# Weighted values as columns in tiles of 32, and the keys' norm moved into the exponential's scale

## The chip, the cores and the metric

The kernel runs on one core of a Trainium2 chip. Its engines are TensorE (PE: matmuls and transposes), VectorE (DVE), ScalarE (ACT), GpSimd (POOL) and the queues that issue DMAs (SP's above all). The metric is the time of one execution on the device in microseconds (us). Before the change it is 1096.64 us, the median of three runs (1096.35 to 1097.41).

## The reference, cut to what matters

Sixteen sequences of 256 tokens with 128 features pass four sublayers: a decaying complex convolution, a mixture of eight experts of which two count, attention with sixteen heads, and a mixture of four layers of which two count. Each stands between layer norms and is added to its input. The change lies in the attention, in the reference:

```python
q = (xn @ w_q).reshape(b, n, HEADS, DIM_HEAD).transpose(0, 2, 1, 3)   # 16 heads of 64
k, v = jnp.split(xn @ w_kv, 2, axis=-1)                                # k, v as q
k = jnp.concatenate([nk, k], axis=2)   # two learned "null" keys and values in front
v = jnp.concatenate([nv, v], axis=2)
q = _l2norm(q) * q_scale
k = _l2norm(k) * k_scale
sim = jnp.einsum('bhid,bhjd->bhij', q, k) * 8.0
sim = sim + dist[None, None] * slopes[None, :, None, None]   # by distance, per head
sim = jnp.where(causal_mask[None, None], neg, sim)
attn = jax.nn.softmax(sim, axis=-1)
out = jnp.einsum('bhij,bhjd->bhid', attn, v)
out = out.transpose(0, 2, 1, 3).reshape(b, n, HEADS * DIM_HEAD)
return out @ w_out
```

## The kernel before, in words

The sixteen sequences are taken in eight groups of two; a group is four tiles of 128 tokens, so 512 tokens. The sublayers of different groups overlap: while group i is in attention, the experts of group i+1 and the start of the convolution of group i+2 are woven in, and the last sublayer of group i-1 runs beside the projections of group i.

What each engine does, and in which order, is written out by hand in tables of step names (PROLOGUE, FIRST, MIDDLE, LAST_L, LAST_A, LAST_F), one list for each engine. `plan` plays them: FIRST once, MIDDLE for five groups, then the three last ones. A step a_ belongs to the attention, l_ to the experts, f_ to the last sublayer, e_ to the convolution, s_ to the setup. Engines meet through semaphores only, and each engine runs strictly down its list: a step that waits holds up all that stand behind it.

The attention of one group has these steps:

- a_m.t (L1693 to L1695 on PE, three matmuls of rounded float32 for each product; L1042 and L1049 on ACT): k and q of token tile t are computed into banks 0 to 2, copied to `unit` and squared into `square`.
- a_ss.t.k: DVE sums the squares by head (L1497), k = 0 for keys and 1 for queries, clamps them (L1500), and POOL raises them to the power of -1/2 (L858, `rnorm`).
- a_u.t.k: DVE scales `unit` by `rnorm` (L1506), for the keys and for the queries.
- a_t.t: PE turns the four parts of `unit` (L1700), ACT copies them into `kT` (L1058) and `qT` (L1060), features by tokens.
- a_v.t: the values into `val`, with a column of ones behind each head.
- a_scores.c: for two heads, PE multiplies keys by queries (L1914 for 256 queries, L1920 for 128), with 64 rows each, two tiles of rows side by side. The result has keys as partitions. ACT takes the exponential with the slope as bias by partition and 8 as the scale (L1108, L1111), POOL multiplies the triangle of the mask (L866). The four buffers of probabilities are `probs`, which lie in `unit` and `square`.
- a_mix.h: for one head, six float32 matmuls of 128x128 (L1955, L1957). The probabilities are the stationary operand and the values with their ones, 128 columns wide, move, so tokens are the partitions of the result, in bank 3. DVE adds the null probabilities to the denominator (L1547), inverts it (L1549) and multiplies (L1551) into `mixed`.
- a_oT.c: PE turns two heads of `mixed` back (L1700), ACT copies them to `outT` (L1129); the last one turns the null probabilities (L1997).
- a_out.h: `outT` times w_out (L2010) plus the null probabilities times w_nv, the null values folded with w_out in the setup (L2011).

In the last group, which has no later one to weave in, the order of heads differs: two sequences one after the other, four heads at a time (L1085 and L1090 on ACT).

Among the other rows that are named: L1837 and L1844 belong to the experts, L2043 to L2113 to the last sublayer, L1635 is DVE's second step on its hidden rows.

## Time and profile before

| | |
|---|---|
| median of three runs | 1096.64 us |
| profiled execution: its span | 1095.0 us |
| PE busy | 1008.8 us (92%), 6854 matmul records |
| DVE busy | 790.9 us (72%) |
| ACT busy | 564.5 us (52%) |
| POOL busy | 571.8 us (52%) |

The profiled execution is one of its own; the span of its trace is 1095.0 us, and the median of the runs is 1.6 us longer. The chain of waits is followed back from the last instruction, at each step to what released it. A record of a matmul begins when it starts and its end is modelled, so records overlap, and what one costs in a row of them is the distance of the starts. One float32 matmul shows as two records, one of rounded float32 as one. The granted clock of PE is 1.00 (2.4 GHz) in all stages shown below.

### The profile page before, as it was taken

What the parts mean: (1) busy time and instruction counts of PE and PEld (TensorE: products, weight loads), DVE (VectorE), ACT (ScalarE), POOL (GpSimd) and SP (SyncE); (2) the same over time, 40 slices, a digit from 0 to 9 for tenths busy, and PEclk for the clock granted to TensorE, in tenths of its full rate; (3) what the DMA queues carried; (4) which work ended last, traced back from release to release, by engine and by line L of the source; (5) the groups of instructions that cost most, each with busy time, mean ns of one, the idle gap of its engine ahead of it and who ended that gap; (6) DMA issues with size and microseconds to landing.
All of it is one profiled execution on the core that took longest, in us unless ns stands there. A gap on an engine that the chain in (4) does not pass through costs nothing.

```text
span 1095.0 us, 19137 instructions
## 1 busy us (share of the span) xinstructions
PE 1008.8 (92%) x6854; PEld 833.2 (76%) x6854; DVE 790.9 (72%) x2565; ACT 564.5 (52%) x1113; POOL 571.8 (52%) x562
## 2 busy tenths in 40 slices
PE   0887999899999999999999999999998999999987
PEld 0565888679975989679886789669896788768965
DVE  5787656977689776888578776887678664793446
ACT  5217653764347542773447542574527653486522
POOL 4127543854457463764637553674637643475523
PEclk9988999999999999999999999999999999999999
DMA  6200000000000000000000000000000000000000
GB/s 161 75 1 10 1 1 1 1 11 1 11 1 1 11 1 11 0 11 1 2 11 1 10 1 11 1 10 1 1 11 1 1 1 1 10 1 1 11 1 10
DMA packets 21870, 11.31 MB, mean 10 GB/s; under 512 B 7440, under 2 KB 21136, under 8 KB 21648
## 3 DMA queue, kind: packets, MB, share of 16 engines
q1 hardware_dynamic: 18064, 8.84, 2.9%
q10 hardware_dynamic: 3712, 1.25, 0.5%
q8 instruction: 55, 0.90, 0.3%
q14 instruction: 39, 0.32, 0.1%
HBM read 7.99 MB, written 2.10 MB: 9 GB/s over the span
## 4 chain that ended last, share of the span: by engine, by line
PE 51%; DVE 29%; POOL 14%; issue 5%; ACT 1%; ACTq 0%; DVEq 0%; POOLq 0%
PE bank L1955 10%; POOL rnorm L858 9%; PE bank L1914 5%; PE bank L1957 5%; PE bank L1700 4%; PE bank L1920 3%; PE bank L1693 3%; DVE unit L1506 3%; DVE sumsq L1497 3%; PE bank L1694 3%; PE bank L1695 3%; PE bank L2107 3%; PE bank L2113 3%; PE bank L1844 2%; PE bank L2010 1%
## 5 line engine op out<-in xcount | busy, mean ns | idle before, releaser
L858 POOL TENSOR_TENSOR rnorm<-sumsq,minus_half 128x16 f32<-128x16 f32 x64 | 185.2, 2921 | 9.4 <-DVE sumsq L1500 9.4
L866 POOL TENSOR_TENSOR unit<-unit,causal 128x256 f32<-128x256 f32 x128 | 89.5, 731 | 100.6 <-ACT unit L1111 87.1
L866 POOL TENSOR_TENSOR square<-square,causal 128x256 f32<-128x256 f32 x128 | 89.4, 730 | 96.3 <-ACT square L1111 87.1
L1914 PE MATMUL bank<-qT,kT 64*128 64x256 f32 x512 | 96.8, 389 | 0.0
L1547 DVE TENSOR_TENSOR denom<-bank,null_sum 128x4 f32<-128x4 f32 x112 | 17.8, 159 | 97.6 <-PE bank L1957 97.4
L1506 DVE TENSOR_TENSOR unit<-unit,rnorm 128x1024 f32<-128x1024 f32 x64 | 79.1, 1240 | 11.3 <-POOL rnorm L858 10.9
L1920 PE MATMUL bank<-qT,kT 64*128 64x128 f32 x512 | 84.1, 284 | 0.8 <-ACT val L1066 0.7
L1497 DVE TENSOR_REDUCE sumsq<-square 128x16 f32<-128x1024 f32 x64 | 77.8, 1215 | 7.4 <-ACT square L1049 7.1
L1955 PE MATMUL bank<-val,unit 128*128 128x128 f32 x512 | 81.4, 282 | 1.3 <-DVE mixed L1551 1.0
L1955 PE MATMUL bank<-val,square 128*128 128x128 f32 x512 | 80.9, 281 | 0.8 <-DVE mixed L1551 0.6
L1129 ACT ACTIVATE qT<-bank 128x512 f32<-128x512 f32 x56 | 33.4, 599 | 93.6 <-PE bank L1700 93.5
L1700 PE MATMUL bank<-ident,unit 128*128 128x128 f32 x520 | 71.3, 286 | 10.8 <-DVE unit L1506 8.3
L1042 ACT ACTIVATE unit<-bank 128x512 f32<-128x512 f32 x128 | 72.2, 601 | 17.3 <-PE bank L1695 14.2
L1920 PEld LDWEIGHTS bank<-qT,kT 64*128 64x128 f32 x512 | 71.1, 187 | 12.1 <-issue 5.1
L1700 PEld LDWEIGHTS bank<-ident,unit 128*128 128x128 f32 x520 | 61.0, 147 | 25.4 <-DVE unit L1506 13.4
L1955 PEld LDWEIGHTS bank<-val,unit 128*128 128x128 f32 x512 | 67.6, 191 | 7.9 <-issue 3.8
L1049 ACT ACTIVATE square<-unit 128x512 f32<-128x512 f32 x128 | 72.9, 630 | 0.1
L1955 PEld LDWEIGHTS bank<-val,square 128*128 128x128 f32 x512 | 68.0, 192 | 5.6 <-issue 2.1
L1914 PEld LDWEIGHTS bank<-qT,kT 64*128 64x128 f32 x512 | 68.8, 187 | 0.5
L1108 ACT ACTIVATE square<-bank,bias_k 128x512 f32<-128x512 f32 x56 | 38.2, 683 | 56.9 <-PE bank L1914 56.9
L2010 PE MATMUL bank<-w_out,qT 128*128 128x128 f32 x512 | 64.3, 279 | 1.4 <-ACT tanh L1121 0.7
L1693 PE MATMUL bank<-w_kv_hi,xaT_hi 128*128 128x512 f32 x128 | 62.1, 485 | 2.5 <-DVE xaT_lo L1402 1.5
(396 smaller groups left out, 2798.0 us busy)
## 6 DMA issues: line engine op xcount, KB each, us to landing
xin<-in_L_attn_x SPq DMA_DIRECT2D x7, 256.0 KB, 2.8
out<-x SPq DMA_DIRECT2D x7, 256.0 KB, 2.2
square<-in_L_attn_w_kv SPq DMA_DIRECT2D x1, 1024.0 KB, 7.3
w_sw<-in_L_ffn_sw_w SPq DMA_DIRECT2D x3, 256.0 KB, 5.0
unit<-in_L_attn_w_q SPq DMA_DIRECT2D x1, 512.0 KB, 6.4
w_out<-in_L_attn_w_out SPq DMA_DIRECT2D x1, 512.0 KB, 4.3
w_ml<-in_L_ffn_ml_w SPq DMA_DIRECT2D x2, 256.0 KB, 5.5
xin<-in_L_attn_x ACTq DMA_DIRECT2D x1, 256.0 KB, 3.0
```

The lines of the kernel that those rows point to most:

```text
L858: pool.tensor_tensor(rnorm[:, k, t, :], sumsq[:, t % 2, k, :], minus_half[:], ALU.pow).then_inc(a_root.sem, 1)
L866: m = pool.tensor_tensor(pd, pd, causal[:].unsqueeze(1).to_broadcast([P, 2, P]), ALU.mult)
L1042: act.activation(unit[:, t % 2, i, :], bank[n % 3][:], ACT.Copy).then_inc(a_took.sem, 1)
L1049: act.activation(square[:, k, :], unit[:, t % 2, k, :], ACT.Square).then_inc(a_sq.sem, 1)
L1497: V.tensor_reduce(sumsq[:, t % 2, k, :], square[:, 2 * k:2 * k + 2, :].rearrange("p j (h d) -> p (j h) d", d=DH), AX_X, ALU.add).then_inc( ...
L1506: V.tensor_tensor(raw, raw, rnorm[:, k, t, :].unsqueeze(2).to_broadcast([P, H, DH]), ALU.mult).then_inc(a_unit.sem, 1)
L1693: mm(dst, left.hi, right.hi, start=True, stop=False)
L1700: last = nc.tensor.transpose(dst[:, t * P:(t + 1) * P], src(t), ident[:])
L1914: return mm(bank[s][:, 2 * P * i:2 * P * (i + 1)], kT[rs, p, 2 * P * b:2 * P * b + P], qT[rs, p, 2 * P * b:2 * P * (b + 1)], start=True, s ...
L1920: return mm(bank[2][:, 2 * P * s + P * i:2 * P * s + P * (i + 1)], kT[rs, p, ts], qT[rs, p, ts], start=True, stop=True)
L1955: last = mm(dst, pr[:, i, 2 * k, :], wide_val(2 * b + k, head), start=True, stop=(k == 0))
L2010: mm(out_bank(g, h)[:, ts], outT[:, c, ts], w_out[:, c, :], start=(c == 0), stop=False)
```

## The change

It has two parts.

The first turns the product with the values around. The values become the stationary operand, 32 of their 64 features at a time, and the probabilities move, so that the result comes out as features by tokens, as `outT` needs it. Four heads stand side by side in the columns of the array. One unit (a_mix.c, eight for a group) does four heads of one sequence. The denominator is a product of its own, with 32 columns of ones, in bank 7; the null keys enter by three full-width matmuls with the turned null probabilities (`null_pT`, now 96 rows: one rounded part twice and one rest) and the matrices `of_head` and `w_nv`. DVE turns the denominators by blocks of 32x32, inverts them, turns them back and multiplies into `outT`. The steps a_oT and the matmuls with w_nv in a_out go, and a step a_nT comes, which turns the null probabilities. Since a unit holds one sequence, all groups now take the heads in the order of the last one, with two exponentials where there was one: four heads of one sequence in place of two heads of both.

The second leaves the keys without their norm. a_k.t turns the raw keys; DVE's clamp of the keys' squares also divides by 64, and POOL's root is then eight times the inverse norm, which the exponential takes as its scale by partition.

The tables of the order are written anew for both parts. Buffers move: the tanh rows go to `conv` and `hid_relu`, `null_pT` to `xaT`. In the setup, null heads are spread over `w_nv` by POOL and ACT, w_out is loaded by eight DMAs in place of one, and null values by three.

```diff
-            def a_units(g, t, k):
-                dve.wait_ge(a_root.sem, a_root.at(g, 2 * t + k + 1))
-                dve.wait_ge(a_took.sem, a_took.at(g, use("m", t, 2 * k + 1) + 1))
-                raw = unit[:, t % 2, 2 * k:2 * k + 2, :].rearrange("p j (h d) -> p (j h) d", d=DH)
-                V.tensor_tensor(raw, raw, rnorm[:, k, t, :].unsqueeze(2).to_broadcast([P, H, DH]), ALU.mult).then_inc(a_unit.sem, 1)
+            def a_units(g, t):
+                dve.wait_ge(a_root.sem, a_root.at(g, 2 * t + 2))
+                dve.wait_ge(a_took.sem, a_took.at(g, use("m", t, 3) + 1))
+                raw = unit[:, t % 2, 2:4, :].rearrange("p j (h d) -> p (j h) d", d=DH)
+                V.tensor_tensor(raw, raw, rnorm[:, 1, t, :].unsqueeze(2).to_broadcast([P, H, DH]), ALU.mult).then_inc(a_unit.sem, 1)
...
+                    V.tensor_scalar(sumsq[:, t % 2, k, :], sumsq[:, t % 2, k, :], 1e-24, 1.0 / 64.0, ALU.max, ALU.mult).then_inc(s.sem, 1)
...
-            def a_t(g, t):
+            def a_k(g, t):
...
+                for k in range(2):
+                    n = use("k", t, k)
+                    pe.wait_ge(a_took.sem, a_took.at(g, use("m", t, k) + 1))
                     free(g, n)
                     turn(bank[n % 3], lambda c: unit[:, t % 2, k, c * P:(c + 1) * P]).then_inc(a_put.sem, 1)
...
-                            last = act.activation(pr[:, j, 0:2, :], k0, ACT.Exp, bias=bias_k0[:, h:h + 1], scale=8.0)
+                            last = act.activation(pr[:, j, 0:2, :], k0, ACT.Exp, bias=bias_k0[:, h:h + 1], scale=by)
...
-                for i in range(2):
-                    b, head = (seq_of(h), head_of(h, i)) if ending(g) else (i, h)
-                    for k in range(2):
-                        dst = bank[pv_bank(g, h)][:, (2 * i + k) * P:(2 * i + k + 1) * P]
-                        last = mm(dst, pr[:, i, 2 * k, :], wide_val(2 * b + k, head), start=True, stop=(k == 0))
-                        if k:
-                            last = mm(dst, pr[:, i, 1, :], wide_val(2 * b, head), start=False, stop=True)
-                last.then_inc(a_pv.sem, 1)
...
+            def a_mix_(g, c):
+                b, q = unit_of(c)
+                quad = [(slice(32 * i, 32 * i + 32), QW * q + i, probs[(2 * c + i % 2) % 4][:, i // 2, :, :]) for i in range(QW)]
+
+                def weigh(dst, left):
+                    for rs, h, pr in quad:
+                        mm(dst[rs, P:2 * P], left(1, h), pr[:, 2, :], start=False, stop=False, skip_group_check=True)
+                    for rs, h, pr in quad:
+                        last = mm(dst[rs, :], left(0, h), pr[:, 0:2, :], start=False, stop=True, skip_group_check=True)
+                    return last
+
+                pe.wait_ge(a_mask.sem, a_mask.at(g, 2 * c + 2))
+                if c:
+                    pe.wait_ge(a_mix.sem, a_mix.at(g, 4 * c - 3))
...
+                elif c and not ending(g):
+                    pe.wait_ge(a_mix.sem, a_mix.at(g, 4 * c))
+                den = bank[7][:, 0:2 * P]
+                parts = [pv_bank(g, c)[:, 2 * P * f:2 * P * (f + 1)] for f in range(2)]
+                mm(den, of_head[:, P * q:P * (q + 1)], null_pT[:, half(b)], start=True, stop=False, skip_group_check=True)
+                for f in range(2):
+                    mm(parts[f], w_nv[:, (2 * q + f) * P:(2 * q + f + 1) * P], null_pT[:, half(b)], start=(f == 0), stop=False,
+                       skip_group_check=True)
+                weigh(den, lambda k, h: ones[:]).then_inc(a_den.sem, 1)
+                for f in range(2):
+                    last = weigh(parts[f], lambda k, h: val[:, 2 * b + k, h, 32 * f:32 * f + 32])
+                last.then_inc(a_pv.sem, 1)
...
+            def a_nT_(g):
...
+                for t in range(T):
+                    for i in range(3):
+                        last = mm(bank[3][32 * i:32 * i + 32, t * P:(t + 1) * P], null_p[:, t, :, :].rearrange("p h n -> p (h n)"), ident[:],
+                                  start=True, stop=True)
+                last.then_inc(a_nT.sem, 1)
...
+                V.transpose(den_rows, bank[7][:, 0:2 * P]).then_inc(s.sem, 1)
+                dve.wait_ge(s.sem, s.at(g, 4 * c + 1))
+                V.reciprocal(recip[:], den_rows[:, 0::32]).then_inc(s.sem, 1)
+                dve.wait_ge(s.sem, s.at(g, 4 * c + 2))
+                V.transpose(rec_cols.rearrange("p (n i) -> p n i", i=32), recip[:].unsqueeze(2).to_broadcast([P, 2 * QW, 32])).then_inc(s.sem, 1)
+                dve.wait_ge(s.sem, s.at(g, 4 * c + 3))
+                dve.wait_ge(a_pv.sem, a_pv.at(g, c + 1))
+                V.tensor_tensor(outT[:, 2 * q:2 * q + 2, half(b)], pv_bank(g, c)[:].rearrange("p (f n) -> p f n", f=2),
+                                rec_cols.unsqueeze(1).to_broadcast([P, 2, 2 * P]), ALU.mult).then_inc(s.sem, 1)
...
-                        mm(out_bank(g, h)[:, ts], outT[:, c, ts], w_out[:, c, :], start=(c == 0), stop=False)
-                    last = mm(out_bank(g, h)[:, ts], null_pT[:, ts], w_nv[:], start=False, stop=True)
+                        last = mm(out_bank(g, h)[:, ts], outT[:, c, ts], w_out[:, c, :], start=(c == 0), stop=(c == 7))
```

The order on PE, in the middle of one group's attention: before, the turn of two finished heads (L1700 with `mixed`), two heads' values (L1955, L1957) and a block of scores.

```order
L1700 MATMUL bank<-ident,mixed 128x128 x4
L1955 MATMUL bank<-val,unit 128x128 x2
L1957 MATMUL bank<-val,unit 128x128
L1955 MATMUL bank<-val,unit 128x128 x2
L1957 MATMUL bank<-val,unit 128x128
L1837 MATMUL bank<-coef,sel 128x512
L1920 MATMUL bank<-qT,kT 128x128
L1914 MATMUL bank<-qT,kT 128x256
```

The same place after the change, a unit (L1926 and L1928 are the two loops of `weigh`, L1948 and L1950 the full-width matmuls) and the scores behind it:

```order
L1948 MATMUL bank<-xaT_hi,of_head 128x256
L1950 MATMUL bank<-xaT_hi,w_nv 128x256 x2
L1926 MATMUL bank<-square,ones 32x128 x4
L1928 MATMUL bank<-square,ones 32x256 x4
L1926 MATMUL bank<-square,val 32x128 x4
L1928 MATMUL bank<-square,val 32x256 x4
L1926 MATMUL bank<-square,val 32x128 x4
L1928 MATMUL bank<-square,val 32x256 x4
L1668 MATMUL bank<-ident,xn 128x128 x4
L1783 MATMUL bank<-ident,pick 8x128 x4
L1895 MATMUL bank<-qT,kT 128x128
```

Four heads of one sequence now stand in one piece, and no turn of `mixed` is left.

The order on DVE at the end of the projections, before: after the last squares, the keys' scaling (L1506) stands in front of the residual of the convolution (L1325, L1330) and the queries' behind it.

```order
L1325 TENSOR_SCALAR ce_rows<-ce_rows,n_c_mv,n_c_rstd 128x128 x4
L1506 TENSOR_TENSOR unit<-unit,rnorm 128x1024
L1325 TENSOR_SCALAR xn<-bank,n_y_mv,n_y_rstd 128x128 x4
L1330 TENSOR_TENSOR x<-xn,xin 128x512
L1314 BN_STATS n_l_six<-x 128x6 x4
L1318 BN_AGGR n_l_mv<-n_l_six 128x2 x4
L1320 TENSOR_SCALAR n_l_var<-n_l_mv 128x4
L1506 TENSOR_TENSOR unit<-unit,rnorm 128x1024
```

After:

```order
L1311 TENSOR_SCALAR ce_rows<-ce_rows,n_c_mv,n_c_rstd 128x128 x4
L1311 TENSOR_SCALAR xn<-bank,n_y_mv,n_y_rstd 128x128 x4
L1316 TENSOR_TENSOR x<-xn,xin 128x512
L1300 BN_STATS n_l_six<-x 128x6 x4
L1304 BN_AGGR n_l_mv<-n_l_six 128x2 x4
L1306 TENSOR_SCALAR n_l_var<-n_l_mv 128x4
L1495 TENSOR_TENSOR unit<-unit,rnorm 128x1024
```

One scaling is gone, and the one of the queries stays behind the residual.

## Rows read from the trace of the kernel before

**Rows 1.** The page's shares of the chain of waits by engine, whole span

```profile
PE 51%; DVE 29%; POOL 14%; issue 5%; ACT 1%; ACTq 0%; DVEq 0%; POOLq 0%
```

**Rows 2.** Busy time by stage: stretch, length, then each engine's busy us (instructions), clock, DMA

```profile
488.00:549.00 61.00, 60.92 (x502) 55.19 (x501) 40.62 (x135) 27.58 (x56) 32.48 (x41) 1.00 0.01 1
549.00:569.30 20.30, 20.19 (x146) 17.90 (x145) 15.90 (x68) 6.36 (x13) 4.18 (x6) 1.00 0.05 15
569.30:613.50 44.20, 40.35 (x200) 27.73 (x199) 39.93 (x112) 33.30 (x62) 33.71 (x17) 1.00 0.02 7
```

**Rows 3.** Pieces of the chain of waits: start us, length us, engine and line

```profile
489.81 0.24 PE bank L1695
490.05 0.89 PE bank L2107 x8
...
1073.02 0.86 PE bank L2044 x2
```

**Rows 4.** Timeline of attention: start us, length us, engine, line, operation, tiles

```profile
506.98 0.71 PE L1955 MATMUL bank<-val,unit 128*128 128x128 f32 x4
...
508.34 0.48 PE L1693 MATMUL bank<-xlT_hi,w_gate_hi 128*128 128x512 f32 x1
```

**Rows 5.** Timeline of PE, end of attention and the norms

```profile
550.90 0.60 PE L1700 MATMUL bank<-ident,mixed 128*128 128x128 f32 x4
551.33 1.28 PE L1844 MATMUL bank<-w_down,unit 128*128 128x128 f32 x10
...
556.32 0.48 PE L2011 MATMUL bank<-w_nv,tanh 32*128 32x128 f32 x2
556.74 2.05 PE L2010 MATMUL bank<-w_out,qT 128*128 128x128 f32 x16
```

**Rows 6.** Timeline of PE, one block of scores and its neighbours

```profile
493.49 0.25 PE L1695 MATMUL bank<-w_router_hi,xlT_lo 128*128 128x8 f32 x1
493.67 0.37 PE L1920 MATMUL bank<-qT,kT 64*128 64x128 f32 x1
493.68 0.48 PE L1914 MATMUL bank<-qT,kT 64*128 64x256 f32 x1
493.88 0.38 PE L1920 MATMUL bank<-qT,kT 64*128 64x128 f32 x2
...
494.98 0.27 PE L1920 MATMUL bank<-qT,kT 64*128 64x128 f32 x1
495.18 1.16 PE L2107 MATMUL bank<-w_sw,mixed 128*128 128x128 f32 x8
```

**Rows 7.** Timeline of PE, projections; in brackets its idle time before

```profile
580.64 1.09 PE L1700 MATMUL bank<-ident,unit 128*128 128x128 f32 x8 [0.51 <-DVE unit L1506]
...
604.34 3.03 PE L2066 MATMUL bank<-xmT,w_ml 128*128 128x512 f32 x6 [1.49 <-DVE mixed L1635]
```

**Rows 8.** Groups of DVE by form: tiles, shapes, count, busy us, mean ns, idle before

```profile
L1506 DVE TENSOR_TENSOR unit<-unit,rnorm 128x1024 f32<-128x1024 f32 x64 | 79.1, 1240 | 11.3 <-POOL rnorm L858 10.9
...
L1551 DVE TENSOR_TENSOR mixed<-bank,recip 128x256 f32<-128x256 f32 x112 | 47.6, 425 | 3.9
...
L1635 DVE TENSOR_TENSOR mixed<-mixed,bank 128x512 f32<-128x512 f32 x32 | 22.0, 687 | 1.1
...
L1549 DVE RECIPROCAL recip<-denom 128x4 f32<-128x4 f32 x112 | 20.2, 180 | 3.9
...
L1547 DVE TENSOR_TENSOR denom<-bank,null_sum 128x4 f32<-128x4 f32 x112 | 17.8, 159 | 97.6 <-PE bank L1957 97.4
```

**Rows 9.** Groups of ACT by form, exponentials of the scores

```profile
L1108 ACT ACTIVATE square<-bank,bias_k 128x512 f32<-128x512 f32 x56 | 38.2, 683 | 56.9 <-PE bank L1914 56.9
...
L1085 ACT ACTIVATE square<-bank,bias_k 128x256 f32<-128x256 f32 x16 | 6.7, 474 | 4.8 <-PE bank L1914 4.8
...
L1090 ACT ACTIVATE unit<-bank,bias_k 128x128 f32<-128x128 f32 x16 | 5.2, 395 | 0.0
```

510 lines of the change are left out of this document (214 added, 296 removed).

## The prediction

> **What bounds the kernel now.** I read the stages first [rows 2], cut at the steps of one iteration of the middle loop. It takes 125.5 us and falls into attention (488 to 549 us; the kernel's first MLP layer is woven into it), a run of layer norms (20 us) and the projections of q, k and v (44 us). In attention TensorE (PE) is busy for 60.92 of 61 us; VectorE (DVE) has 40.6, ScalarE (ACT) 27.6, GpSimd (POOL) 32.5. In the projections DVE has 39.9 of 44.2 us and PE 40.4. The chain of waits says the same of the whole: PE carries 51% of it, DVE 29%, POOL 14% [rows 1]. So in attention a microsecond that PE gains or loses counts nearly in full, in the projections only PE's gaps can be won, and in the norms a ping-pong of DVE and POOL sets the pace. There are eight groups of two sequences, so each term is worked out for one group and taken eight times.
>
> The unit of all PE terms is the pass. A float32 matmul shows as two passes; one over 512 columns takes 0.86 / 2 = 0.43 us, one over 128 columns 0.89 / 8 = 0.11 us, so one over 256 about 0.215. A pass of rounded float32 over 512 columns takes 0.24 [rows 3].
>
> **What PE loses.** A head's weighted values, six float32 matmuls, stand from 506.98 to 508.34: 1.36 us [rows 4], sixteen heads 21.8. A turn of the result (four transposes) takes 551.33 - 550.90 = 0.43 us [rows 5]; six of them lie in attention, 2.6. In sum 24.4 us. Three more turns and four matmuls with w_nv (0.42 each, from 556.32 to 556.74 [rows 5]) go from the stretch of norms: 3.0 us.
>
> **What PE gains.** Eight units. In each, three full-width matmuls of rounded float32 over 256 columns (no such row; half of 0.24, so 0.12; bounds 0.11, since no pass in these rows is shorter, and 0.215): 0.36. Then three times the same block, which I call w: four heads side by side in column tiles of 32, each with a float32 matmul over 128 and one over 256 columns. One after the other its passes take 8 x 0.11 + 8 x 0.215 = 2.6 us; four abreast 0.65. No row shows column tiles. The nearest are the scores, with two row tiles of 64: exactly the same set of passes, 2.6 us in a row and 1.30 two abreast. They run from 493.67 to the last start at 494.98 plus 0.11, which is 1.42 us, and their second matmul starts 0.01 us after the first while the first's own second pass comes only at 493.88 [rows 6]. The tiles really run beside each other, at 92% of the ideal. I take w = 0.65 x 1.42 / 1.30 = 0.71, bounds 0.65 and 2.6. Around the scores PE has a hole of 0.07 us before (493.49 + 0.11 to 493.67) and 0.09 behind (495.09 to 495.18) [rows 6]; I take 0.1 for each change of tile size, two in a unit. A unit is 0.36 + 3 x 0.71 + 0.2 = 2.69 us, eight are 21.5. The twelve small matmuls that turn the null probabilities come in threes abreast, 4 x 2 x 0.11 + 0.2 = 1.1. Together 22.6 against 24.4: -1.8 us for a group, -14 for all. At w = 0.65 it would be -26, and at w = 0.79 nothing.
>
> The Trainium skill ("TensorE: Matmul & The Clock Gate", Measured speedup vs the span model) gives 2.38 times for three column tiles. Scaled to four (an estimate, 3.17 times) w would be 0.82, the PE term +7 us and the total 1075. No run here shows column tiles yet.
>
> **Projections.** DVE loses four of the eight scalings by the norm, 4 x 1.24 = 5.0 us for a group [rows 8], and the transposes of k no longer wait for POOL's root. But DVE's time isn't what counts, PE's gaps are, and they come to 44.2 - 40.35 = 3.9 us [rows 2]. The largest wait for DVE: 0.51 for a scaled half in front of its transposes, and 1.49 for a hidden part of the second layer, which stands on DVE behind the scalings [rows 7]. The last link stays, q's scaling in front of q's transposes, and DVE reaches it one scaling, 1.2 us, earlier. I take -2.5 us for a group (bounds 0 and -3.9): -20.
>
> **Norms.** The chain there starts at DVE's last multiplication and passes through units of norm work that don't change. PE loses 3.0 us in it but is only partly waited for. I take -1 (bounds 0 and -3): -8.
>
> **What I cost at nothing.** On DVE a unit has two stream transposes (no such row; bounds 0.18, the reciprocal, and 0.69, a 128x512 operation; I take 0.43, the 128x256 one from the bank), a reciprocal and a multiplication of 0.69: 1.73 us in place of 2 x (0.16 + 0.18 + 0.43) = 1.54 for two heads [rows 8]. That is +1.6 us for a group beside 20 free ones. Two waits come with it. A unit's first matmul waits for the multiplication of the unit before, because both write bank 3, and for its first transpose, because the denominators have bank 7 alone; the turn of the normed input, which shares bank 7, waits likewise. All of PE's queue stands behind such a wait. The multiplication is through about 1 us after a unit's last pass, and scores of 1.5 us stand between any two units but the last two, where half of the down projection does. If that cover went, each unit would cost up to 1 us, 64 in all. On ACT a pair of heads now takes 4 x 0.474 + 4 x 0.395 = 3.5 us of exponentials, before 2 x (0.683 + 0.474) = 2.3 [rows 9], +9 us for a group. Even without the copies of the turned result, which go, that is 37 of 59 us. The scale by partition I take as free, since the bias is already read that way (bounds 0 and 0.1 us for each of 64 exponentials in a group). The prologue loses eight small matmuls and gets seven DMAs and some POOL and ACT work ahead of a wait that comes later: 0, bounds -2 and +2.
>
> **Sum.** -14 - 20 - 8 = -42 us. The profiled span is 1095.0, so 1053; the median of the runs lies 1.6 above it, which gives 1054.6. From here on differences under 0.2% (2 us) are no change, as a measurement can't tell them.
>
> **Rivals.**
> A, two abreast. The passes of a float32 matmul are two instructions, and a second pass must follow the first in its own tile. If PE keeps the order of passes within a row group, tile 1 starts only when tile 0's second pass has, and so on: never more than two at work, w = 1.3. A unit is then 4.46 us, eight 35.7, the PE term +12.4 for a group, with the other gains +8.9 and 71 in all: 1168. It decides from w = 0.79 for PE and 0.93 for the whole. For it: the scores cross row groups, where this can't be seen; all four column tiles share all rows. Against it: in the scores the passes of two matmuls are interleaved, not in order [rows 6]. The Trainium skill's rule speaks for it ("TensorE: Matmul & The Clock Gate", Part 3, The mechanism): matmuls start and end in program order and only weight loads are pulled ahead, when their row group differs. The scores here break it by 0.2 us, across row groups.
> B, a floor per pass. Away from the scores no pass takes under 0.11 us, whatever its size. If 16 passes cost 16 x 0.11, w is 1.8, a unit 5.96, the PE term +24.4, in all +167: 1264. Against it: 16 passes of the scores take 1.42, that is 0.09, with the array full. A floor of 0.06 would give w = 0.96 and +6 in all.
> C, no overlap at all: w = 2.6, a unit 8.36, the PE term +43.6, in all 1417. Against it: row tiles do overlap [rows 6].
> D, the exponentials take PE's place. The scores of a pair wait for all exponentials of the pair before; if PE arrives 0.7 us early at each of eight, +5.6 for a group and +45 in all eat the gain: 1099, next to no change. For it: +1.2 us for a pair on ACT. Against it: a pair has 59 / 8 = 7 us, and a loop of 1.4 us of scores and 3.5 of exponentials is shorter.
>
> **How the numbers follow.** Four abreast has 0.56; its own range is 1031 (w = 0.65, which gives -12 more, and all of the gaps, -11 more) to 1090 (w = 0.85, +27, and a third of the gaps, +9). A has 0.20, B and C together 0.12, D and a small floor 0.12, of which 0.05 is faster, 0.05 no change and 0.02 slower. Predicted is the likeliest, 1054.6, as 1054. The range leaves out B and C and the slow end of A: 1031 to 1172. Faster is 0.56 + 0.05 = 0.61, the same 0.05, slower 0.20 + 0.12 + 0.02 = 0.34.
>
> **What would show it.** The w blocks: twelve or more passes starting within 0.7 us, the first passes of four tiles within a few hundredths. Under A starts come in steps of 0.11 and 0.215 with two open at a time. Attention would take about 59 us and the projections 41.5. PE stays near 99% busy in attention; if it falls and the longest waits are PE's scores for ACT, D holds. The prediction is wrong if w is above 0.93, or if the projections keep their 44 us.

## The result and the profile after

The changed kernel takes 1107.1 us (median of four runs, 1104.4 to 1108.9) against 1096.5: slower by 1%, ratio 1.0092 with an interval of 1.0076 to 1.0108. The profiled execution spans 1104.2 us where that of before spans 1095.0. The forecast was 1054. One of the eleven executions of a later kernel, the column tiles alone, took 3268.5 us where the others took 1092 to 1096, and stands in no comparison.

PE's work fell as planned, and more. On the page of the profile before, it is 1008.8 us busy (92%); after, first lines and chain shares (engine, busy us, share of the span, instructions; then the chain by engine):

```profile
span 1104.2 us, 22172 instructions
PE 964.8 (87%) x8405; PEld 738.5 (67%) x8405; DVE 778.6 (71%) x2393; ACT 617.7 (56%) x1288; POOL 578.9 (52%) x570
PE 50%; DVE 28%; ACT 11%; issue 5%; POOL 5%; ACTq 0%; DVEq 0%; POOLq 0%
```

So PE works 44 us less and stands idle 53 us more (139 for 86). ACT had 1% of the chain [rows 1]; it has 11%.

One unit on PE, from the timeline (start, length, engine and line, tiles, shapes, count); the rows of before for one head are [rows 4], for row tiles [rows 6]:

```profile
516.79 0.28 PE L1948 MATMUL bank<-xaT_hi,of_head 96*128 96x256 f32 x1
516.91 0.40 PE L1950 MATMUL bank<-xaT_hi,w_nv 96*128 96x256 f32 x2
517.24 0.43 PE L1926 MATMUL bank<-square,ones 128*32 128x128 f32 x8
517.48 0.61 PE L1928 MATMUL bank<-square,ones 128*32 128x256 f32 x8
517.91 0.40 PE L1926 MATMUL bank<-square,val 128*32 128x128 f32 x8
518.13 0.61 PE L1928 MATMUL bank<-square,val 128*32 128x256 f32 x8
518.56 0.40 PE L1926 MATMUL bank<-square,val 128*32 128x128 f32 x8
518.78 0.61 PE L1928 MATMUL bank<-square,val 128*32 128x256 f32 x8
519.33 0.33 PE L1668 MATMUL bank<-ident,xn 128*128 128x128 f32 x1
```

A block of sixteen passes begins every 0.65 us (517.91 - 517.24 = 0.67, then 0.65), and the trace has the first passes of its four tiles within 0.02 us of each other. The four tiles work abreast with nothing lost. The unit takes 519.33 - 516.79 = 2.54 us.

Busy time by stage (stretch, length, busy us and instructions of PE, PEld, DVE, ACT, POOL, clock, DMA). The first three stretches are those of [rows 2] in one middle group: attention, norms, projections. The last six cut two middle groups at the first sum of squares, the first scores and the last scores, as I do from here on. This second cut calls the stages projections, scores and norms; what follows the last scores (the last units, the down projection) is in its norms:

```profile
490.30:556.00 65.70, 61.87 (x741) 48.96 (x739) 45.86 (x124) 35.88 (x84) 33.31 (x41) 0.97 0.02 6
556.00:573.50 17.50, 15.39 (x106) 13.20 (x105) 12.89 (x59) 6.00 (x13) 4.19 (x6) 1.00 0.00 0
573.50:614.80 41.30, 37.18 (x185) 25.46 (x184) 34.60 (x102) 30.16 (x55) 32.60 (x17) 1.00 0.03 8
...
445.50:495.80 50.30, 46.70 (x244) 33.90 (x242) 38.84 (x117) 36.87 (x67) 39.01 (x22) 0.97 0.02 6
495.80:543.00 47.20, 44.88 (x561) 35.23 (x561) 34.91 (x102) 28.26 (x69) 24.45 (x31) 1.00 0.01 2
543.00:573.50 30.50, 26.89 (x243) 21.77 (x241) 21.37 (x77) 9.33 (x21) 8.00 (x11) 0.94 0.03 10
573.50:622.80 49.30, 45.18 (x243) 32.68 (x241) 38.81 (x117) 36.95 (x67) 38.26 (x22) 1.00 0.02 6
622.80:669.90 47.10, 44.79 (x559) 35.15 (x560) 34.81 (x102) 28.30 (x69) 24.45 (x31) 1.00 0.01 2
669.90:698.60 28.70, 25.37 (x244) 20.90 (x242) 21.50 (x78) 9.33 (x21) 8.01 (x11) 1.00 0.04 11
```

By the first cut the projections take 41.3 us, as forecast (44.2 before); but attention takes 65.7 for 61. The second cut, which ends the projections only at the first scores, shows that little was won: 50.3 and 49.3 us, before 50.1. The work that the first cut counts as projections ended earlier, but the scores did not begin earlier. Two things more stand in these rows. PE is idle over 2 us in a stage of scores where it was never idle. And the same stage takes 1 to 1.8 us longer where PE's granted clock is 0.97 or 0.94 than where it is 1.00: 3.4 us at 1.2 GHz, which the middle groups of before did not have. The second of the two groups, all at full clock, takes 125.1 us (before 125.7), the first, with both low stretches, 128.0.

The same three stretches of before, for comparison with all that follows:

```profile
443.60:493.70 50.10, 46.26 (x247) 33.15 (x245) 42.89 (x120) 38.19 (x70) 38.45 (x22) 1.00 0.02 6
493.70:540.90 47.20, 47.12 (x394) 42.43 (x395) 34.49 (x117) 20.29 (x43) 23.98 (x32) 1.00 0.01 1
540.90:569.30 28.40, 28.29 (x211) 25.37 (x208) 19.27 (x79) 8.95 (x18) 7.95 (x11) 1.00 0.04 10
```

Counted from the starts of the groups' first sum of squares, the first group lost 2.1 us, the five middle ones 1.6 in all, the last stretch (last attention and the end) 5.8, and the last but one won 0.4. ce_rows and x4m are normed rows that PE has to turn, the first at the end of the norms, the second early in the projections; `unit` from L1451 is the experts' hidden rows. What PE waits for, in total, times, longest (its own list; in the list of before ce_rows and null_p do not stand among the 21 longest, and x4m has 5.2 us):

```profile
PE bank L1820 <- DVE ce_rows L1334: 12.2, 10, 3.1
PE bank L1820 <- DVE x4m L1334: 11.5, 6, 2.2
PE bank L1805 <- DVE unit L1451: 10.7, 6, 3.1
...
PE bank L1916 <- ACT null_p L1092: 7.3, 2, 5.0
```

And ACT's exponentials, by form (count, busy us, mean ns, idle before), to be held against [rows 9]:

```profile
L1114 ACT ACTIVATE square<-bank,bias_k,rnorm 128x256 f32<-128x256 f32 x128 | 65.8, 571 | 58.9 <-PE bank L1889 58.9
L1120 ACT ACTIVATE unit<-bank,bias_k,rnorm 128x128 f32<-128x128 f32 x128 | 52.8, 479 | 0.0
```

571 and 479 ns where 474 and 395 stood. A piece of the chain of waits (start, length, engine and line) shows how that reaches PE:

```profile
525.90 0.66 PE bank L1889 x5
...
529.71 0.70 ACT unit L1120 x2
530.40 0.50 ACT mixed L1042
...
531.53 0.68 DVE unit L1446
532.21 0.37 DVE mixed L1514
...
532.84 0.46 DVE mixed L1518
...
533.32 0.70 DVE qT L1521
534.02 0.14 issue
534.16 0.36 PE bank L1948
```

The scores end at 526.6; then ten exponentials (eight, and two more for the steep heads 0 and 1), 3.8 us; behind them on ACT the tanh of the MLP layer; behind that DVE's two hidden steps, and behind those DVE's four steps of a unit; only then does PE get bank 3. This unit's multiplication is through 3.9 us after the unit's last pass. The prediction had about 1 us there; in a middle group of this trace four of the eight units have that, the other four 1.9 to 3.9.

### The profile page after: what moved, and what is told of

The parts are those of the page before. It is cut to its first block, busy times and chain, and to the rows that moved or that the text cites. A ratio compares the mean times of both kernels' runs of the same rounds, so it can differ in the third digit from the quotient of the medians.

```text
span 1104.2 us, 22172 instructions
## 1 busy us (share of the span) xinstructions
PE 964.8 (87%) x8405; PEld 738.5 (67%) x8405; DVE 778.6 (71%) x2393; ACT 617.7 (56%) x1288; POOL 578.9 (52%) x570
## 4 chain that ended last, share of the span: by engine, by line
PE 50%; DVE 28%; ACT 11%; issue 5%; POOL 5%; ACTq 0%; DVEq 0%; POOLq 0%
PE bank L1928 5%; PE bank L1668 5%; PE bank L1661 4%; PE bank L1663 3%; PE bank L1662 3%; PE bank L1926 3%; PE bank L1889 3%; PE bank L2061 2%; PE bank L2020 2%; ACT unit L1120 2%; PE bank L2067 2%; POOL rnorm L870 2%; ACT unit L1114 2%; DVE sumsq L1483 2%; PE bank L1812 2%
## 5 line engine op out<-in xcount | busy, mean ns | idle before, releaser
L878 POOL TENSOR_TENSOR square<-square,causal 128x256 f32<-128x256 f32 x128 | 97.5, 785 | 92.8 <-ACT square L1120 92.8
L1114 ACT ACTIVATE square<-bank,bias_k,rnorm 128x256 f32<-128x256 f32 x128 | 65.8, 571 | 58.9 <-PE bank L1889 58.9
L1046 ACT ACTIVATE xaT_hi<-bank 128x256 fp32r<-128x256 f32 x16 | 6.0, 384 | 145.7 <-PE bank L1820 145.7
L1668 PE MATMUL bank<-ident,unit 128*128 128x128 f32 x520 | 67.9, 277 | 10.6 <-DVE unit L1495 8.9
L1668 PEld LDWEIGHTS bank<-ident,unit 128*128 128x128 f32 x520 | 58.3, 142 | 24.4 <-DVE unit L1495 11.0
L1114 ACT ACTIVATE unit<-bank,bias_k,rnorm 128x256 f32<-128x256 f32 x96 | 51.5, 575 | 27.3 <-PE bank L1889 27.3
L1965 PE MATMUL bank<-w_out,qT 128*128 128x128 f32 x512 | 59.9, 276 | 1.1 <-DVE qT L1521 1.1
L1965 PEld LDWEIGHTS bank<-w_out,qT 128*128 128x128 f32 x512 | 58.4, 192 | 2.2 <-DVE qT L1521 1.7
L1441 DVE SCALAR_TENSOR_TENSOR unit<-mixed,bank 128x512 f32<-128x512 f32 x35 | 24.0, 685 | 46.2 <-ACT mixed L1042 46.0
L1495 DVE TENSOR_TENSOR unit<-unit,rnorm 128x1024 f32<-128x1024 f32 x32 | 40.3, 1259 | 21.3 <-POOL rnorm L870 21.0
L1514 DVE STREAM_TRANSPOSE mixed<-bank 128x256 f32<-128x256 f32 x64 | 28.5, 446 | 37.0 <-PE bank L1928 36.7
L1120 ACT ACTIVATE unit<-bank,bias_k,rnorm 128x128 f32<-128x128 f32 x128 | 52.8, 479 | 0.0
```

The source lines that it names most:

```text
L878: m = pool.tensor_tensor(pd, pd, causal[:].unsqueeze(1).to_broadcast([P, 2, P]), ALU.mult)
L1114: last = act.activation(pr[:, j, 0:2, :], k0, ACT.Exp, bias=bias_k0[:, h:h + 1], scale=by)
L1120: last = act.activation(pr[:, j, 2, :], bank[2][:, 2 * P * s + P * j:2 * P * s + P * (j + 1)], ACT.Exp, bias=bias_k1[:, h:h + 1], scale=by)
L1668: last = nc.tensor.transpose(dst[:, t * P:(t + 1) * P], src(t), ident[:])
L1965: last = mm(out_bank(g, h)[:, ts], outT[:, c, ts], w_out[:, c, :], start=(c == 0), stop=(c == 7))
```

## The experiments

The theories after the result. **Theory 1**: the exponentials are what PE waits for, because each is longer (1a, the scale by partition) and there are twice as many (1b). **Theory 2**: banks 3 and 7 come back through DVE's queue. **Theory 3**: PE's new gaps bring its clock down. All runs are compared with the kernel before on the same chip (1096.5 to 1096.9).

### Constant scale in the changed kernel

```
-  act.activation(pr[:, j, 0:2, :], k0, ACT.Exp, bias=bias_k0[:, h:h + 1], scale=by)
+  act.activation(pr[:, j, 0:2, :], k0, ACT.Exp, bias=bias_k0[:, h:h + 1], scale=8.0)
```

> The changed kernel, but the exponentials take the constant 8.0 as their scale instead of a value by partition. The norm of the keys is left out of the result by that; every instruction stays. If the scale by partition lengthens the exponentials and they are what PE waits for (theory 1a), the rows on 128x256 go back from 0.57 to about 0.475 us and those on 128x128 from 0.48 to 0.39; at 64 exponentials in each of eight groups, up to 0.095 x 512 = 49 us come back, since only part of them is on the path I expect 20 to 45: 1062 to 1087. If the single banks 3 and 7 with their hand-over through DVE's queue are the cause (theory 2), or the clock alone (theory 3), the exponentials get shorter and the time moves by under 8 us from 1107.

Measured: 1088.9 us (ratio 0.9929, 0.9916 to 0.9942), 18.2 below the changed kernel. The same rows:

```profile
L1113 ACT ACTIVATE square<-bank,bias_k 128x256 f32<-128x256 f32 x128 | 54.3, 484 | 74.5 <-PE bank L1887 74.4
L1118 ACT ACTIVATE unit<-bank,bias_k 128x128 f32<-128x128 f32 x128 | 41.7, 398 | 0.0
```

So the scale by partition costs 0.08 to 0.09 us an instruction, 49 us of ACT's time (617.7 us busy, here 568.5), and 18 of them reach the end. Theory 1a holds in kind; the size is just under the 20 to 45 that it expected.

### The column tiles alone

```
-  V.tensor_tensor(raw, raw, rnorm[:, 1, t, :]...)            # q alone, once for a token tile
+  V.tensor_tensor(raw, raw, rnorm[:, k, t, :]...)            # k and q, as before
+  ... ACT.Exp, bias=bias_k0[:, h:h + 1], scale=8.0)
```

> The first part of the change by itself: column tiles as changed, but the keys are scaled by DVE as before, and the exponentials have the constant scale 8.0. Theory 1a: as the experiment with the constant scale, plus what the second part had won in the projections, 44.2 - 41.3 = 2.9 us and the norms' share of it, so 15 to 25 us more than that one and under or near the 1096 of before (1080 to 1100). Theory 2 or 3: 1107 plus 20, about 1120 to 1130.

Measured: 1093.3 us (0.9975, 0.9965 to 0.9986): faster than before by 3.6 us (2.7 by the ratio). A middle group:

```profile
443.00:493.40 50.40, 45.44 (x242) 32.73 (x240) 42.93 (x120) 37.22 (x68) 38.72 (x22) 1.00 0.02 6
493.40:539.80 46.40, 44.78 (x559) 35.16 (x560) 35.82 (x104) 22.59 (x69) 25.43 (x32) 1.00 0.01 2
539.80:567.70 27.90, 25.32 (x244) 20.85 (x242) 20.77 (x75) 8.54 (x21) 7.95 (x11) 1.00 0.04 11
```

PE works 2.3 us less among the scores and 3.0 less behind them, and the stages are 0.8 and 0.5 us shorter; the projections are 0.3 longer, with x4m waited for 2.15 us where it was 0.88. Of 5.3 us taken off PE 1.3 are time. That is the net of this version, in which the exponentials are split and DVE's unit is longer as well. It lies in the wide range of theory 1a, but only 4.4 us above the experiment before, not 15 to 25. And with a constant scale the second part is worth 1093.3 - 1088.9 = 4.4. I had given it 28 us. (8 of them, the norms', belong by the prediction's own reason, less work for PE there, to the first part, which leaves 20.) With its real scale it costs 1107.1 - 1093.3 = 13.8.

### Scale by partition alone, in the kernel before

```
-  ... ACT.Exp, bias=bias_k0[:, h:h + 1], scale=8.0)
+  ... ACT.Exp, bias=bias_k0[:, h:h + 1], scale=eight[:])
```

> The kernel before, with the same number 8.0 read as a scale by partition from a column of memory in all its exponentials. Theory 1a expects each exponential 0.09 us longer here too, in a kernel whose ACT has room: before it is busy 27.6 of 61 us in attention and the exponentials are 32 to 36 a group outside the last one, so 3 us more in 61 and a time within 4 us of before (1096 to 1101). If the exponentials are not longer here, then the lengthening in the changed kernel has another cause (the memory behind the scale, or two engines reading one bank).

Measured: 1102.6 us (1.0054, 1.0041 to 1.0067), 5.7 over before: more than expected. The row of [rows 9] with 683 ns reads here:

```profile
L1110 ACT ACTIVATE square<-bank,bias_k,eight 128x512 f32<-128x512 f32 x56 | 43.3, 773 | 53.6 <-PE bank L1916 53.6
```

0.09 us each, with one and the same number behind the scale: the price is the operand's, not the data's. Even an ACT that is 52% busy over the whole is not free where PE is at 99%.

### The second part alone, and the split alone

The keys without their norm in the kernel before (first edit), and the kernel before with only its exponentials split (second):

```
+  by = rnorm[:, 0, 2 * b, h:h + 1]
+  act.activation(probs[h % 4][:, b, 0:2, :], k0[:, b, :, :], ACT.Exp, ..., scale=by)      # for b in 0, 1
...
+  act.activation(probs[h % 4][:, b, 0:2, :], k0[:, b, :, :], ACT.Exp, ..., scale=8.0)     # for b in 0, 1
```

> The second part of the change by itself, in the kernel before: keys transposed without their norm, DVE scales q alone, the exponentials take the norm by partition and so are split by sequence (four instructions for a head where there were two); the weighted values stay as before, a head at a time. If the prediction's terms for projections and norms hold (-2.5 and -1 us a group), 1097 - 28 + 6 for the scale by partition = 1075. If what the constant-scale experiments say holds (second part worth only 4.4 us, 1093.3 to 1088.9), 1097 - 4 + 6 plus whatever the split exponentials cost where PE is at 99%: 1098 to 1108.

> The kernel before with its exponentials split by sequence outside the last group (four of half the size for a head pair's two), constant scale, nothing else. It separates the two costs of the second part: with the scale by partition alone the time rose 5.7 us, with the whole second part 24.4. ACT's fixed cost is about 0.27 us an instruction by the sizes of before (0.683 for 512 columns, 0.474 for 256, 0.395 for 128), so a pair costs 1.2 us more. If the number of exponentials is what counts: 1106 to 1116. If it is only the scale, paid on twice as many instructions: 1096 to 1100, and the rest of the 24.4 is 12 us for the scale and the new order of the projections.

Measured: 1121.1 us (1.0222, 1.0209 to 1.0235) for the second part alone, 24.4 over before and far outside both expectations; 1105.5 us (1.0079, 1.0066 to 1.0092) for the split alone, 8.8 over before, just under what the count of exponentials should do. The scale on the unsplit exponentials (5.7) and the split (8.8) add up to 14.5; the other 9.9 are the scale on the exponentials that the split adds and the new order of the projections, which no run here takes apart. Where the projections' gain went, on DVE (in brackets its idle time and what ended it), first before, then the second part alone:

```profile
465.11 1.22 DVE L1506 TENSOR_TENSOR unit<-unit,rnorm 128x1024 f32<-128x1024 f32 x1
466.71 1.23 DVE L1506 TENSOR_TENSOR unit<-unit,rnorm 128x1024 f32<-128x1024 f32 x1 [0.38 <-POOL rnorm L858]
```

```profile
473.63 0.69 DVE L1648 TENSOR_TENSOR mixed<-mixed,bank 128x512 f32<-128x512 f32 x1
475.79 1.23 DVE L1519 TENSOR_TENSOR unit<-unit,rnorm 128x1024 f32<-128x1024 f32 x1 [1.47 <-POOL rnorm L857]
```

The scaling that is gone had lain beside POOL's next root. Without it DVE waits 1.47 us for the same root. Over the whole run DVE's idle time in front of its scalings is 11.3 us before and 22.0 here. The stages of this kernel:

```profile
450.50:499.90 49.40, 46.15 (x246) 33.16 (x245) 38.72 (x116) 37.93 (x70) 38.32 (x22) 1.00 0.02 6
499.90:550.40 50.50, 47.47 (x395) 42.45 (x395) 34.86 (x117) 30.17 (x73) 25.15 (x31) 1.00 0.00 1
```

0.7 us won in the projections (DVE has 4.2 less work there), 3.3 lost among the scores, with ACT at 30.17 us for 20.29.

### PE's work and DVE's hand-over, each by itself

Both start from the column tiles alone. The first leaves out the second half of each head's columns, the second leaves out the two stream transposes, so that the denominators are not the right ones:

```
-  for f in range(2):
+  for f in range(1):
       last = weigh(parts[f], ...)
...
-  V.transpose(den_rows, ...); V.reciprocal(recip[:], ...); V.transpose(rec_cols, ...)
+  V.reciprocal(recip[:], bank[7][:, 0:2 * P:32])
```

> The column tiles alone (keys scaled by DVE), with the second half of the head's columns left out of the weighted values: one block of 0.65 us less in each of 64 units, 5.2 us less PE work a group, 41.6 in all. If PE still sets the pace of attention as before, the time falls by 30 to 42 us from 1093.3, to 1051 to 1063. If the first part's own gain has already used up what PE could give (the prediction's failed step as I now see it), it falls by under 12: 1081 to 1093.

> The column tiles alone, with DVE's work for a unit cut from four steps to two (the two stream transposes are left out, so the denominators are read from the wrong places): 1.73 us become 0.2 + 0.69, banks 7 and 3 come free 0.8 us earlier. Theory 2 (hand-over of the banks through DVE): the gaps before units close, 0.9 us a group, and DVE's later steps come 0.8 us earlier each, in all 8 to 25 us: 1068 to 1085. If the hand-over is covered by scores as the prediction assumed: 1089 to 1093.

Measured: 1077.8 us (0.9816, 0.9798 to 0.9833) and 1083.3 us (0.9879, 0.9864 to 0.9893). 41.6 us less of PE's work (64 blocks of 0.65) bring 15.5, between the two expectations: PE's time still counts, at 37%. The transposes are 0.45 us each, so DVE has 0.9 us less in each of 64 units (its busy time falls from 815.8 to 759.3); that brings 10.0, which is in theory 2's range. Neither engine alone is the bound any more; they take turns. Theory 2 holds as a part.

### The clock

```
   def f_clock(g):
-      for _ in range(5):
+      for _ in range(12):
           mm(bank[6][:], w_kv.hi[:, 0:P], w_kv.hi[:, 0:N], start=True, stop=True)
```

> The changed kernel with twelve filler matmuls in place of five at the one place where PE has stood 2.15 us for the transposed x4m since the change (0.88 before it); seven more at 0.23 are 1.6 us and fit into the gap. Theory 3 (PE's new gaps let the clock fall to 1.2 GHz): the 3.4 us at half clock that follow in most middle groups go away, up to 1.7 us for each of five to seven groups, 1096 to 1101. If the clock does not matter, or falls for the gaps elsewhere, 1106 to 1109.

Measured: 1106.3 us (1.0085, 1.0067 to 1.0104): nothing. The projections of the middle groups are all at full clock now (49.3 us), but the low clock turns up in the norms of four middle groups instead. Later I filled a gap there as well, the one ahead of ce_rows, in the kernel of the next section (the changed kernel with the null exponential first), with ten fillers of 0.12 us:

> The changed kernel with the null exponential first in the last two groups (1096.5 so far), with twelve filler matmuls in place of five ahead of the wait for x4m and ten of 0.12 us ahead of the wait for ce_rows (1.35 us in the middle groups). Twelve fillers alone moved nothing: the 3.4 us at half clock only came one gap later. Theory 3: with both gaps filled they go from the five middle groups, 1 to 1.9 us each by the groups of the changed kernel that have one against those that have none, so 1089 to 1094, and the runs lie closer together than the 6.5 us of the kernel without fillers. If the clock isn't worth anything: 1095 to 1098.

Measured: 1097.1 us (0.9993, 0.9981 to 1.0005) against 1096.5 without fillers: nothing again in the median; three middle groups still have some us at 1.2 GHz in the norms. But the gap that I filled is not the one in front of them. In the trace of the changed kernel the low stretch of the norms begins behind PE's wait for the experts' hidden rows, 17 us ahead of the wait for ce_rows (first the matmul that waited, then a stretch around it, with the clock third from the end; within it the granted clock is 0.50 from 545.5 us on, to 548.9):

```profile
544.93 0.49 PE L1805 MATMUL bank<-coef,sel 40*128 40x512 f32 x1 [1.51 <-DVE unit L1451]
534.00:548.00 14.00, 12.34 (x157) 9.23 (x161) 9.37 (x17) 8.13 (x20) 9.86 (x14) 0.91 0.01 2
```

That wait is still 1.51 us in the filled kernel, and its three low stretches in the norms begin behind it again. Such a wait alone is not enough: the middle groups of the changed kernel have ten waits of 1.5 to 2.2 us (this one and x4m) and four low stretches, each beginning within 0.8 us behind one. With a constant scale, in the two experiments above, this wait is 0.78 us, and no middle group has a low stretch in its norms; in a version below that makes it 2.35 us, three have one. The twelve executions of the filled kernel also fall into two sets, five at 1093.4 to 1093.9 us with mean clocks of 0.980 to 0.983 and seven at 1096.9 to 1099.6 with 0.974 to 0.978; the five are in theory 3's range. So filling gaps has not shown theory 3, and has not tested it at this wait. What speaks for it is inside one kernel: groups with and without the low clock differ by 1 to 1.8 us.

### The null exponential first

The one wait that I had nowhere. In the last group of the changed kernel ACT makes the null probabilities behind the ten exponentials of the first scores, and PE, which must turn them before the first unit, has nothing ahead of that:

```profile
1009.51 0.84 ACT L1120 ACTIVATE unit<-bank,bias_k,rnorm 128x128 f32<-128x128 f32 x2
1010.19 0.36 ACT L1092 ACTIVATE null_p<-null_s 128x128 f32<-128x128 f32 x1
```

```profile
1010.60 1.93 PE L1916 MATMUL bank<-ident,null_p 128*32 128x128 f32 x24 [5.00 <-ACT null_p L1092]
```

The same turn takes 1.93 us here, nearly twice its time at full clock (1.07 at 1003.26 in the kernel of this experiment). Before, the null probabilities were turned last. The edit, in the last two groups' tables:

```
 DVE  -... a_u.3 ... f_out.0 f_out.1 f_out.2 a_nexp f_out.3 a_nT    +... a_u.3 a_nexp ... f_out.0 f_out.1 f_out.2 f_out.3 a_nT
 ACT  -... a_v.3 a_scores.0 a_nexp a_nT                              +... a_v.3 a_nexp a_scores.0 a_nT
```

> The changed kernel with one thing moved in the last two groups: the exponential of the null logits, with DVE's two steps ahead of it, stands before the exponentials of the first pair of heads instead of behind them, and before DVE's sums of the second layer. In the trace of the changed kernel PE waits there for null_p, 5.00 us in the last group and 2.35 in the one before, a wait that the prediction has nowhere. If it is on the path, 5 to 8 us come back (1099 to 1102); if the exponentials then only wait elsewhere (theory 1), under 2.

Measured: 1096.5 us (1.0001, 0.9988 to 1.0014), 10.6 below the changed kernel, more than the 7.3 us of waiting and more than expected. With this alone the whole loss against before is gone. The last stretch falls from 152.6 to 144.5 us (before: 146.8), the group ahead of it from 126.6 to 124.8. Twelve runs of this kernel lie between 1094.1 and 1100.6, with mean granted clocks of 0.98 to 0.968: the three highest times have the three lowest clocks.

### Versions

All keep the column tiles, DVE's scaling of the keys and the constant scale. The first goes back to one exponential for both sequences of a head and takes the units in pairs behind four heads:

```
+  more = [... for i in range(4)]          # four more buffers of probabilities, in mixed
   def unit_of(g, c):
-      return divmod(c, U // SEQ)
+      return divmod(c, U // SEQ) if ending(g) else divmod(c, SEQ)[::-1]
```

> A version that keeps the column tiles and the DVE-scaled keys, and gives the scores back their old form outside the last group: one exponential for both sequences of a head (512 and 256 columns, 2.3 us a pair of heads instead of 3.5), constant scale, and the column-tiled units taken in pairs behind the scores of four heads; eight buffers of probabilities. Theory 1 (time of exponentials is what PE waits for): attention falls to under 60 us, in all 1055 to 1080, below before. Theory 2 (hand-over of banks 3 and 7 through DVE): two units stand right behind each other here with no scores between, so it should be slower than the experiment with tiles only, by up to 1 us for each of 32 pairs.

Measured: 1097.3 us (1.0006, 0.9997 to 1.0015). Theory 1b expected more; slower than the tiles alone, by 4.0 us, is what theory 2 expected. The first group took 106.9 us for 109.9, the last but one 124.8 for 125.6, but the middle ones 2 longer: stages of scores as long as in the column tiles alone (46.4 us), two units more behind them. With half the exponentials that stage keeps its length, so it is not their number that sets it there once the scale is constant.

> The column tiles alone (constant scale, DVE scales the keys), with the null exponential first in the last two groups as in the experiment on it, and three steps moved in the middle groups: DVE starts the norm of the first MLP layer before the last unit instead of behind it, and adds the second layer's result 12 us earlier, in a wait for the tanh; POOL takes that layer's root two steps sooner. Where DVE's queue order is the bound in the norms (PE waits 1.35 us for ce_rows and 2.15 for x4m there in each middle group), 1.5 to 3 us a group go, with the null wait 12 to 22 in all: 1071 to 1081. If the chain of norms is bound otherwise, only the null wait's 5 to 7: 1086 to 1089.

The second takes the column tiles alone, the null exponential first, and moves DVE's norm steps:

```
 DVE  -a_mix.4 l_hc.1 l_hg.4 a_mix.5 l_hc.2 l_hc.3 l_hu.4 a_mix.6 f_end a_mix.7 l_dstats.0
      +a_mix.4 l_hc.1 f_end l_hg.4 a_mix.5 l_hc.2 l_hc.3 l_hu.4 a_mix.6 l_dstats.0 a_mix.7
 POOL -a_scores.6 a_scores.7 f_end_stats l_dstats.0                 +f_end_stats a_scores.6 a_scores.7 l_dstats.0
```

Measured: 1097.9 us (1.0002, 0.9987 to 1.0016), from 1091.8 to 1099.3. Wrong: the last group won its 5.9 us (142.1 for 148.0), the middle ones lost. f_end in its new place holds up l_hg and all behind it:

```profile
541.76 0.79 PE L1801 MATMUL bank<-coef,sel 40*128 40x512 f32 x1 [2.35 <-DVE unit L1450]
```

That wait was 0.78 us in the column tiles alone. The next version meant the double exponentials for the first and last but one group, but by an oversight used them in the middle ones too, whose order is made for the other form:

> The version before it, with one exponential for both sequences of a head in the first and the last but one group (8 buffers of probabilities, as in the version that had this in all groups but the last). In that version those two groups took 106.9 and 124.8 us where the column tiles alone took 109.9 and 125.6, and the middle ones were 2 us longer. So 2 to 5 us under the version before it.

Measured: 1173.9 us (1.0711, 1.0697 to 1.0725); PE waits 2.0 to 3.7 us for POOL's masks four times in a middle group. It says what a unit in the wrong place costs, and that its first and last groups were right (106.6, 124.1, 142.3 us). Put together as meant, and with DVE's and POOL's norm steps back where the changed kernel has them:

```
+  def by_seq(g):
+      return g not in (0, G - 2)
```

> The column tiles alone, constant scale, the null exponential first in the last two groups, and one exponential for both sequences of a head in the first and last but one group, this time in these two alone (in the earlier try all middle groups had it too, with an order made for the other form). By the groups measured so far: 83.1 us of prologue, 106.6, five of 124.9 to 125.2, 124.1, 142.2 and 1.7 around the span: 1082, range 1079 to 1088.

Measured: 1083.5 us (0.9876, 0.9862 to 0.9891), as added up. Then only l_dstats.0 ahead of a_mix.7, with f_end left behind a_mix.6:

> The version before it, and in the middle groups DVE starts the norm of the first MLP layer before the last unit (POOL takes the second layer's root two steps sooner for it), with nothing else moved. Then POOL's 0.8 us for the root lies beside the unit. PE waits less for ce_rows, 0.5 to 1.3 us a group: 1076 to 1080; if PE's queue is what sets the end of these norms, as before.

Measured: 1080.5 us (0.9852, 0.9839 to 0.9864), 3.0 less and just above the expected range. The wait for ce_rows is 0.73 us for 1.35. Last the twelve fillers:

> The version before it, with twelve fillers for five ahead of the wait for x4m. If the clock falls on that gap: 1 us less for each middle group, 3 to 5 in all; if it falls one gap later, no change.

Measured: 1079.2 us (0.9839, 0.9827 to 0.9852): 17.4 us, or 1.6%, below the kernel before, and the best here. The mean granted clock of the profiled run is 0.983 for 0.972, no middle group has a stretch at 1.2 GHz any more, and the spread of five runs is 1.4 us. The time moved by 1.3 us where 3 to 5 were expected, and the two intervals overlap. In the profiled executions the projections of the last group are 1.1 us longer (53.7 for 52.7), so the fillers have a price too. Here the clock is worth little. A middle group of it:

```profile
437.60:488.00 50.40, 47.02 (x251) 34.04 (x249) 42.87 (x120) 37.23 (x67) 38.79 (x22) 1.00 0.02 6
488.00:534.40 46.40, 44.78 (x561) 35.18 (x561) 35.87 (x104) 22.55 (x69) 26.37 (x33) 1.00 0.01 2
534.40:562.00 27.60, 25.59 (x244) 20.92 (x241) 20.79 (x76) 8.62 (x21) 7.00 (x10) 1.00 0.04 10
```

## Why the prediction was wrong

**Right: the block w.** Forecast 0.71 us, measured 0.65, its lower bound; rivals A, B and C are refuted by the first rows shown above, and the estimate of 0.82 was too high as well. The unit is 2.54 us for 2.69.

**Right: PE's work.** Forecast -1.8 us a group in attention and -3.0 in the norms, 38 in all. Measured -2.3 and -3.0 in a middle group, and 44.0 over the span.

**Wrong: what that work is worth.** The step that failed is "So in attention a microsecond that PE gains or loses counts nearly in full". PE was at 99% because the orders of DVE, POOL and ACT had been fitted to keep just ahead of it; that is my reading of the tables, the runs show what follows. When PE has 5.3 us less to do in a middle group, 1.3 are time; a further 5.2 bring 37%. The rest turns into gaps, those of [rows 7] and new ones: ce_rows, x4m, the experts' hidden rows, bank 3. So a gain on PE does not count nearly in full; whether a loss on it would was not tested.

**Wrong: the exponentials at nothing.** "The scale by partition I take as free" was given bounds of 0 and 0.1 us for 64 exponentials a group; the upper end is right by size (0.09) and I took the lower. The exponentials are 68 a group with those of the steep heads. It costs 18.2 us here and 5.7 in the kernel before. The Trainium skill ("ScalarE: Activation LUTs", What ACT_TABLE_LOAD costs) says that each operand read by partition adds about 93 ns to an activation; the traces agree (90 ns at 512 columns in the kernel before, 87 at 256 in the changed one). That page spoke against the change, and I had not weighed it. That the bias is read that way already was no reason: the price is paid for each operand.

**Wrong: the projections at -2.5 us a group and the norms at -1.** At the cut that counts, the first scores, the projections won 0.7 us (second part alone) and the norms 0.5 (column tiles alone). Of the 5.0 us forecast, 4.2 were really gone from DVE in this stage (42.89 to 38.7), but I took them off the waits of [rows 7] without asking what else DVE had been waiting for: where a scaling of 1.24 us is gone, the wait for POOL's root is 1.47 for 0.38. I had read the projections' end at their last pass and not at the first scores.

**Missing: the wait for null_p.** The change moves the turn of the null probabilities from the end of attention to its start. I counted its 1.1 us on PE and not what PE waits for: in the last two groups an exponential that ACT reaches only behind the first ten of the scores. It costs 10.6 us.

**The waits on banks 3 and 7 at nothing.** The cover was taken to be whole; "up to 1 us a unit, 64 in all" was the other end. "The multiplication is through about 1 us after a unit's last pass" holds for half of a middle group's units only (1.9 to 3.9 us for the others), about where DVE's unit stands behind a tanh that waits for exponentials. A hand-over shorter by 0.9 us brings 10.0 us, so the cover has holes.

**Right: the prologue.** The first sum of squares starts at 82.6 us for 82.4.

**Rival D** (0.12) had the right engine and nearly the right time, 1099, but the time by luck. By its own sign it fails: PE's scores waiting for ACT's exponentials are not among the longest waits (2.8 us in all). Its reason against ("a loop of 1.4 us of scores and 3.5 of exponentials is shorter" than 7 us) looked at ACT's time and not at ACT's order: what hurts is what stands behind the exponentials.

**The range and the signs.** That 1107 lies within 1031 to 1172 is luck too: the upper part of the range was there for rival A, which did not happen. And neither of the two signs of being wrong came: w is 0.65, and the projections left their 44 us by the cut that the prediction used. Both watched terms that were taken for uncertain, not the step from less work to less time.

The sum by experiments: without the scale's 18.2 us and the null wait's 10.6 the changed kernel would be at 1078, if they add. They were not run together in it, and they may overlap: with a constant scale the null wait itself is 5.5 us for 7.3. The forecast was 1054.6. The remaining 24 us or more are gains that did not come. The second part brought 4.4 us at a constant scale, of the 20 forecast for the projections; the first brought 3.6, with the null wait still in it, of the 22 forecast for attention and norms. How much of the rest is the clock stays open: the fillers moved its low stretches and did not remove them, until the last version, where the time fell by 1.3 us.

## What to carry to other kernels

An engine at 99% next to engines at 50 to 70% need not be the only bound: their orders can be fitted to each other. Price work taken from it at full only until the next engine's queue order is the wait, and walk that queue in the trace: each gap that opens has a name one step back. When a step moves from the end of a stage to its start, look at what it reads and where that stands in its maker's queue, in the first and last groups too, which have tables of their own. Name a sign of being wrong for the step from work to time as well, not for the sizes alone. And an operand by partition is not free because another operand is read that way.

## What was not expected of the hardware

- Column tiles lose nothing: 16 passes of four heads in 0.65 us, where they would take 2.6 in a row, while row tiles of 64 run at 92% [rows 6]. The weight loads between them do not lengthen the block.
- A scale read by partition costs 0.09 us an exponential, beside a bias that is read so as well.
- In the middle groups of the changed kernel 3.4 us at 1.2 GHz (granted clock 0.94 to 0.97 over the stage) follow some of PE's waits of 1.5 and 2.15 us, not all: four of ten. With the wait of 2.15 filled, they follow the one of 1.5 in four groups instead of two. Runs of one and the same kernel differ by 6.5 us (1094.1 to 1100.6) with mean clocks from 0.98 to 0.968.
